# Upsampling matmuls on eight tiles of 32 rows by 64 columns, in staggered steps

## What is computed

```python
def _L1_conv_ref(input, bias, up_filter, down_filter):
    out = input + bias[None, :, None, None]
    out = _sep_upfirdn(out, up_filter * UP, UP, 1, UP_PAD)
    out = jax.nn.leaky_relu(out, NEG_SLOPE) * FLRELU_SCALE
    out = _sep_upfirdn(out, down_filter, 1, DOWN, DOWN_PAD)
```

## Time and profile before

| | |
|---|---|
| median of 3 runs | 7979.34 us (7979.21 to 7982.24) |
| profiled execution | 7980.32 us |
| its span, first to last instruction | 7978.5 us |
| mean granted TensorE clock | 0.959 of full speed |
| busy: PE, VectorE, ScalarE, POOL | 92%, 80%, 51%, 32% |
| resample stage | from about 1741 us to the end |

### The profile page before, as it was taken

The page is one execution under the profiler, slowest core; times in us unless marked ns, Lnnn a source line. Parts: engine busy times, 40 slices in busy tenths (PEclk is TensorE's granted clock), DMA queues, the critical chain, the costliest instruction groups (busy, mean ns, idle before and its releaser), DMA issues.

```text
span 7978.5 us, 374577 instructions
## 1 busy us (share of the span) xinstructions
PE 7350.8 (92%) x151493; PEld 6596.8 (83%) x151493; DVE 6373.1 (80%) x12643; ACT 4069.3 (51%) x8046; POOL 2543.3 (32%) x3076
## 2 busy tenths in 40 slices
PE   6888867049999999999999999999999999999999
PEld 3444442039999999999999999999999999999999
DVE  8999950878888888888888888888888888888887
ACT  0000002336666666666666666666666666666666
POOL 0000000014444444444344444444444444444443
PEclk9999978569999999999999999999999999999999
DMA  7777734013333333333333333333333333333332
GB/s 293 300 292 300 290 123 178 1 35 92 91 91 92 91 91 92 91 91 92 91 91 92 92 91 91 92 91 90 92 92 90 92 92 91 91 92 91 91 92 86
DMA packets 1253328, 925.41 MB, mean 116 GB/s; under 512 B 175312, under 2 KB 1224912, under 8 KB 1234384
## 3 DMA queue, kind: packets, MB, share of 16 engines
q1 hardware_dynamic: 1243920, 890.10, 34.4%
q10 hardware_dynamic: 9344, 34.61, 1.6%
HBM read 621.50 MB, written 303.04 MB: 116 GB/s over the span
## 4 chain that ended last, share of the span: by engine, by line
PE 78%; DVE 0%; ACT 0%; POOL 0%; issue 0%; DMA 0%; DVEq 0%; POOLq 0%
PE bank L991 38%; PE bank L980 29%; PE bank L985 9%; PE bank L1044 2%; DVE leaky L1152 0%; ACT slope_t L1091 0%; DMA low<-conv_dram 0%; POOL low_f L959 0%; DVE x_sum L1135 0%; ACT dn L1117 0%; POOL low_d L956 0%; POOL lift L962 0%; POOL img L947 0%; ACT low_v L1100 0%; ACT res L1108 0%
## 5 line engine op out<-in xcount | busy, mean ns | idle before, releaser
L1152 DVE SCALAR_TENSOR_TENSOR leaky<-bank,slope_t 128x512 f32<-128x512 f32 x4096 | 2637.2, 685 | 576.8 <-ACT slope_t L1091 512.5
L1091 ACT ACTIVATE slope_t<-bank 128x512 f32<-128x512 f32 x4096 | 2219.8, 597 | 1699.5 <-PE bank L985 1699.5
L980 PE MATMUL bank<-up_t,up 64*128 64x133 f32 x16384 | 2187.8, 273 | 2.1 <-DVE leaky L1152 1.9
L985 PE MATMUL bank<-up_t,up 64*128 64x133 f32 x16384 | 2188.1, 273 | 0.0
L991 PE MATMUL bank<-down_t,leaky 128*64 128x67 f32 x65536 | 2086.2, 222 | 0.0
L980 PEld LDWEIGHTS bank<-up_t,up 64*128 64x128 f32 x16384 | 2010.6, 187 | 3.1 <-issue 1.7
L985 PEld LDWEIGHTS bank<-up_t,up 64*128 64x128 f32 x16384 | 2007.9, 187 | 0.0
L991 PEld LDWEIGHTS bank<-down_t,leaky 128*64 128x64 f32 x65536 | 1999.0, 137 | 0.1
L1144 DVE COPY up<-bank 128x512 f32<-128x512 f32 x2048 | 1318.7, 685 | 628.1 <-PE bank L985 628.1
L956 POOL TENSOR_TENSOR low_d<-low_v 128x252 f32<-128x252 f32 x512 | 310.9, 607 | 4081.5 <-ACT low_v L1100 4081.5
L985 PE MATMUL bank<-up_t,x_sum 64*128 64x133 f32 x8192 | 1521.7, 299 | 0.0
(11 more groups left out here) (154 smaller groups left out, 3446.4 us busy)
## 6 DMA issues: line engine op xcount, KB each, us to landing
img<-in_x SPq DMA_DIRECT2D x1024, 256.0 KB, 2.8
out<-res SPq DMA_DIRECT2D x1024, 256.0 KB, 2.2
rows_in<-in_x SPq DMA_DIRECT2D x48, 4224.0 KB, 13.9
rows_in<-in_x SPq DMA_DIRECT2D x16, 4096.0 KB, 13.7
conv_dram<-conv ACTq DMA_DIRECT2D x64, 512.0 KB, 4.1
xb<-conv_dram SPq DMA_DIRECT2D x8, 4096.0 KB, 13.3
low<-conv_dram SPq DMA_DIRECT2D x512, 64.0 KB, 2.3
xx<-conv_dram SPq DMA_DIRECT2D x2, 2048.0 KB, 10.1
```

Of the source, the lines that this page charges most:

```text
L980: return pe.matmul(acc[:, 0:UP_REACH], src, up_t[0:HALF, 0:UP_REACH], start=first, stop=False, skip_group_check=True)
L985: return pe.matmul(acc[:, UH - UP_REACH:UH], src, up_t[HALF:P, UH - UP_REACH:UH], start=first, stop=False, skip_group_check=True)
L1091: nc.scalar.activation(slope_t[e][i][:], u2_acc[e][i][:], ACT.Copy, scale=SLOPE * GAIN).then_inc(slope_out, 1)
L1152: v.scalar_tensor_tensor(out=leaky[1 - m % 2][:, e, i].rearrange("p k w -> p (k w)"), in0=u2_acc[e][i][:], scalar=GAIN, in1=slope_t[e][i][ ...
```

## The change

Upsampling goes to eight tiles: four row tiles of 32 rows, each with two column tiles of 64. Row tile r reaches only the outputs from 2 x 32 r - 5 to 2 x 32 (r + 1) + 5, so 69 or 74 columns. The work of a slot is laid out as twelve steps: six items (two banks of the first upsampling, four of the second) with two halves each. In step t, row tile rt works on half-item (t - 3 rt) mod 12, so that the four row tiles are in four different banks. From step 2 on, a step waits for the end of the step before the last (`up_step`). The bilinear pass becomes two 64-column tiles over 128 rows, half of them zero, behind all of upsampling; d2_acc and b1_acc move to banks 1 and 7. The first downsampling of e = 0 goes ahead of the second downsampling. ScalarE takes over the copy of u1_acc[0]; slope_t of e = 0 goes ahead of low_v, and the copy stands behind all slope_t. On VectorE x_sum moves from the head of the slot to its end.

```diff
-UP_REACH = 2 * HALF + 5
+T = 32
+NT = P // T
+UP_REACH = [(max(0, 2 * T * r - 5), min(UH, 2 * T * (r + 1) + 5)) for r in range(NT)]
...
-                low = [sb(f"low{i}", [HO, LOWS, WO]) for i in range(2)]
+                low = [sb(f"low{i}", [P, LOWS, WO]) for i in range(2)]
...
-                d2_acc = bank[0]
-                b1_acc = bank[6][:, 0:LOWS * WO]
+                d2_acc = bank[1]
+                b1_acc = bank[7][:, 0:LOWS * WO]
...
+                ITEMS = ((1, 0), (2, 0, 0), (2, 1, 1), (2, 0, 1), (2, 1, 0), (1, 1))
+                STEPS = 2 * len(ITEMS)
...
+                    def rise(acc, src, rt, first):
+                        a, b = UP_REACH[rt]
+                        for c in range(2):
+                            mm = pe.matmul(acc[cols(c), a:b], src[:, cols(c)], up_t[T * rt:T * (rt + 1), a:b],
+                                           start=first, stop=False, skip_group_check=True)
+                        return mm
...
+                        used = set()
+                        for t in range(STEPS if has(u, 0) or has(u, 1) else 0):
+                            if t >= 2:
+
+                                pe.wait_ge(up_step, cnt(u, r, m, 0, per=STEPS) + (t - 1))
+                            for rt in range(NT):
+                                at = (t - 3 * rt) % STEPS
+                                item, half = ITEMS[at // 2], at % 2
+                                rows = slice(T * rt, T * (rt + 1))
+                                if item[0] == 1 and has(u, 0):
+                                    i = item[1]
+                                    if not used & {(1, 0), (1, 1)}:
+                                        pe.wait_ge(x_summed, cnt(u, r, m, 1))
...
+                                    mm = rise(u1_acc[i][:, half * UH:(half + 1) * UH], x_sum[p][rows, half, i, :], rt, item not in used)
+                                    used.add(item)
+                                if item[0] == 2 and has(u, 1):
+                                    e, i = item[1:]
+                                    if item not in used:
+
+                                        if i == 0:
+                                            pe.wait_ge(u1_out0, cnt(u, r, m, 0))
+                                        else:
+                                            pe.wait_ge(u1_out1, cnt(u, r, m, 0))
+                                        if after(u, 2):
+                                            pe.wait_ge(leaky_out, cnt(u, r, m, -2, per=4) + (2 * e + i + 1))
+                                    mm = rise(u2_acc[e][i][:, half * UW:(half + 1) * UW], up1[1 - p][rows, i, e, half * P:(half + 1) * P],
+                                              rt, item not in used)
+                                    used.add(item)
+                            mm.then_inc(up_step, 1)
...
+                            for c in range(2):
+                                mm = pe.matmul(b1_acc[cols(c)], const("lin")[:, cols(c)], low[(m // 2 + 1) % 2][:].rearrange("p c w -> p (c w)"),
+                                               start=True, stop=True)
+                            mm.then_inc(b1_mm, 1)
+                        if has(u, 2):
+                            pe.wait_ge(leaky_out, cnt(u, r, m, -1, per=4))
+                            if after(u, 3):
                                 pe.wait_ge(d1_out, cnt(u, r, m, -3, per=2) + 1)
...
+                            first_down(0, p)
...
-                            for e in range(2):
-                                first_down(e, p)
+                            first_down(1, p)
...
+                        if has(u, 0):
+                            act.wait_ge(up_step, cnt(u, r, m, 1, per=STEPS))
+                            nc.scalar.activation(up1[p][:, 0].rearrange("p e h -> p (e h)"), u1_acc[0][:], ACT.Copy).then_inc(u1_out0, 1)
...
+                    for i in range(2):
+                        v.memset(low[i][HO:P], 0.0).then_inc(padded, 1)
...
+                        if has(u, 0):
+                            v.wait_ge(up_step, cnt(u, r, m, 1, per=STEPS))
+                            v.tensor_copy(up1[m % 2][:, 1].rearrange("p e h -> p (e h)"), u1_acc[1][:]).then_inc(u1_out1, 1)
```

More of the change, by code:

```diff
@@ L976, in _ @@
                     pe.wait_ge(ready, 2 + 2 * FT)
-                    def upper(acc, src, first):
-                        return pe.matmul(acc[:, 0:UP_REACH], src, up_t[0:HALF, 0:UP_REACH],
-                                         start=first, stop=False, skip_group_check=True)
-                    def lower(acc, src, first):
-                        return pe.matmul(acc[:, UH - UP_REACH:UH], src, up_t[HALF:P, UH - UP_REACH:UH],
-                                         start=first, stop=False, skip_group_check=True)
+                    pe.wait_ge(padded, 2)
                     def down(acc, src, j, first):
@@ L994, in cols @@
                         return slice(HALF * c, HALF * (c + 1))
-                    def first_up(e, i, p, half, first):
-                        tile = (upper, lower)[half]
-                        return tile(u1_acc[i][:, e * UH:(e + 1) * UH], x_sum[p][HALF * half:HALF * (half + 1), e, i, :], first)
-                    def second_up(e, i, p, half, k, first):
-                        tile = (upper, lower)[half]
-                        return tile(u2_acc[e][i][:, k * UW:(k + 1) * UW],
-                                    up1[p][HALF * half:HALF * (half + 1), i, e, k * P:(k + 1) * P], first)
+                    def rise(acc, src, rt, first):
[4 more added lines that the diff above has]
+                        return mm
                     def first_down(e, p):
@@ L1028, in slot @@
-                        if has(u, 1):
-                            pe.wait_ge(u1_out, cnt(u, r, m, 0, per=2))
-                            for e in range(2):
-                                if after(u, 2):
-                                    pe.wait_ge(leaky_out, cnt(u, r, m, -2, per=4) + 2 * (e + 1))
-                                for k in range(2):
-                                    second_up(e, 0, 1 - p, 0, k, k == 0)
-                                    mm = second_up(e, 1, 1 - p, 1, k, k == 0)
-                            mm.then_inc(u2_half, 1)
+                        used = set()
@@ L1063, in slot @@
                             if has(u, 0):
[L1065 removed]
+                                pe.wait_ge(u1_out1, cnt(u, r, m, 1))
                             elif after(u, 4):
@@ L1075, in slot @@
                         if has(u, 2):
-                            pe.wait_ge(leaky_out, cnt(u, r, m, -1, per=4))
+                            if after(u, 3):
+                                pe.wait_ge(d1_out, cnt(u, r, m, -2, per=2))
                             if group:
                                 pe.wait_ge(b1_out, cnt(u, r, m, 4, of=2))
-                            for e in range(2):
-                                first_down(e, p)
+                            first_down(1, p)
                     schedule(pe, slot)
@@ L1094, in slot @@
                         p = m % 2
+                        if has(u, 1):
+                            act.wait_ge(up_step, cnt(u, r, m, 1, per=STEPS))
+                            slope(u, r, m, 0)
                         if m % 2 == 0 and has(u, -2):
@@ L1153, in slot @@
                                                            scalar=GAIN, in1=slope_t[e][i][:], op0=ALU.mult, op1=ALU.max).then_inc(leaky_out, 1)
+                        if has(u, -1):
+                            n = (m + 1) % STEP
+                            v.wait_ge(lifted, cnt(u, r, m, 1 + 2, of=2))
+                            v.wait_ge(biased, cnt(u, r, m, 2))
+                            for e in range(2):
+                                for i in range(2):
+                                    c0 = cnt(u, r, m, 1, per=4) + (2 * e + i)
+                                    cf = coef[:, bass.ds(c0, 1)] if u is None else coef[:, c0:c0 + 1]
+                                    ins = v.scalar_tensor_tensor(out=x_sum[n % 2][:, e, i, :], in0=lift[n // 2][:, 2 * (n % 2) + e, :],
+                                                                 scalar=cf, in1=img[n % 2][:, e, i, :], op0=ALU.mult, op1=ALU.add)
+                            ins.then_inc(x_summed, 1)
                     schedule(v, slot)
```

67 lines of the change are left out of this document (14 added, 53 removed).

## The result

The changed kernel takes 13,873.08 us (median, 13,851.46 to 13,929.94) against 7980.79 us for the kernel before beside it: ratio 1.739, with a 95% interval of 1.734 to 1.745. The forecast was 12,050 us with a range of 9,900 to 13,900. The direction and the likeliest case were right, the size is 1,820 us too small, and the time lies only 27 us inside the upper edge of the range; one of its four runs, at 13,930 us, lies outside.

A forecast was written before the change was run, and what follows sets the result against it. TensorE was taken to bound the kernel, and after the change the refetching of its loop body: 1782.7 us outside the loop + 16 straight-line + 254 rounds x 40.4 us = 12,060, predicted as 12,050 us, range 9,900 to 13,900.

The forecast's parts named there:

- the likeliest case: TensorE's loop: body fetched anew each round, rounds of 34.8 to 51.2 us, own range 10,600 to 13,900 us; chance 0.86.
- The body: TensorE's loop body grows to 2,400 instructions, touches 10 or 11 packets, doesn't fit and is fetched anew every round.
- Price of a packet: TensorE's instruction fetch: 3.2 us on demand, 3.1 to 3.7 us from one packet to the next, 3.4 taken.
- The round: Four pairs on TensorE: 6.4 us demand fetches, 2.6 cut packets, 29.4 whole packets, 2.0 x_sum; 40.4 us instead of 24.4.
- the clock as a risk at the upper edge: TensorE might fall to the lower clock while it starves for instructions, which lies at the range's upper edge.
- The order on VectorE: x_sum last in VectorE's slot: chain of 4.8 us, 1.7 us a pair unhidden; 0.5 a pair taken beside the fetches.
- rival B: TensorE's body stays held and the new x_sum chain sets the pace: 9,500 or 8,180 us; chance 0.11.
- The waits between steps: Upsampling on TensorE: two steps need at least 0.46 us, 0.23 each, 2.8 us for twelve, as much as now.
- the array's 1.5 us: Upsampling's lower bound, step wait always met: twelve steps in 1.5 us for 2.7, at best 1.2 us a pair less.
- the bound of 3.3 us: Upsampling's upper bound a pair: a further 0.05 us for every one of some 10 added register computations.
- Rival C: TensorE's body stays held and it runs at array speed: a round 19.7 us, 6,790 us in all; chance 0.02.
- What was costed at nothing: Other engines and order: ScalarE 17.6 us a round, VectorE 17.0, bilinear pass 0.43 as before, downsampling order with 2 us left.

The follow-up runs named there:

- b_body8: The kernel before, with TensorE's loop body at eight slots instead of four, 2,382 instructions for 1,194; 8,612 us, ratio 1.079.
- a_body2_xfirst: The changed kernel with TensorE's loop body at two slots (1,205 instructions) and x_sum back at the head of VectorE's slot; 8,459 us, ratio 1.060.
- b_xlast: The kernel before, with x_sum moved from the head of VectorE's slot to its end; 11,061 us, ratio 1.385.
- a_body2: The changed kernel with TensorE's loop body at two slots instead of four, 1,205 instructions, one low buffer; 10,855 us, ratio 1.359.
- a_waitprev: The changed kernel with two-slot body and x_sum at the head, each step waiting for the one just before it; 13,386 us, ratio 1.677.
- a_xfirst: The changed kernel with x_sum back at the head of VectorE's slot, four-slot body kept; 13,527 us, ratio 1.694.
- a_pool_early: Changed kernel, two-slot body, x_sum at head, step waits in mid-step, GpSimd's bias for two pairs before widening, img loaded before low; 8,054 us, ratio 1.009.

## Why the prediction was right, and where its size was off

**The body.** Right. The forecast 2,400 instructions are 2,407; 10 or 11 packets touched are 11 a round; about 2,800 packets and 45 MB are 2,819 and 46.19 MB. That the body is the cause is shown from both sides: with a short one the change has no packets and takes 3,018 us less, or 5,068 less with x_sum at the head (13,527 to 8,459), and the old kernel gets them with a long body. That the store is smaller than 11 packets was assumed with no row near 11, and it held; seven stay and eleven don't, and where between them the limit lies was not measured.

**Price of a packet.** The 3.2 us on demand fit: the first stall behind the branch has a median of 3.19 us (nine rounds in ten: 2.9 to 3.6) in the change and 3.6 in b_body8. The second stall is shorter, 1.9 us in the mean, behind some work between the two (1.32 us in the round shown). The 3.1 to 3.7 us from one packet to the next were too short: over the loop the middle interval is 3.96 us, only one in twenty is under 3.47, and 72% are over 3.7. In b_body8, where PE rarely stands, one interval in ten is under 3.1 us, so 3.5 is no floor of the fetch.

**The round** is the step that failed in size, 47.5 us for 40.4. The term was 8.4 whole packets at the longer of 3.4 us and what they run, 2.6 us on average, 3.9 in downsampling, both at full clock. By that term PE works 9.4 x 2.6 = 24.4 us a round and stands for 16.0. In the round shown it works 34.7 us and stands for 13.0. So the standing was put 3 us too high and the running 10 us too low, and part of the error cancelled.

PE's stalls brought the clock down to 0.77: downsampling's 96 instructions took 4.50 us, 256 at that pace 256 x 4.50/192 = 6.0 us, well over the 3.4 of a fetch. There a packet waits for PE and no longer PE for the packet. The same four pairs in a_body2_xfirst, at clock 1.00, have 2 x 13.08 x 0.987 = 25.8 us of busy PE. The other 8.9 us are slow running, 10.9 are "issue" (9.6 and 1.3) and 2.2 the wait for x_sum; the sum is 47.8, the round 47.67. The prediction named the clock as a risk at the upper edge and gave it no term. That the time still fell inside the range is in part luck, since no sum with the clock in it set the upper bound.

How much of the 8.9 us is the clock can be read from the windows of this round: the time from the branch to the first fall, then its three stretches at the lower level, 1.2 GHz.

```profile
7819.56:7825.62 6.06, 1.95 (x77) 1.69 (x74) 0.60 (x3) 1.32 (x3) 0.00 (x0) 1.00 0.37 103
...
7825.62:7835.86 10.24, 7.87 (x203) 6.84 (x204) 4.14 (x7) 2.85 (x6) 2.54 (x4) 0.50 0.01 3
7842.68:7846.10 3.42, 3.42 (x102) 3.23 (x92) 2.34 (x4) 2.28 (x5) 1.04 (x1) 0.50 0.02 5
7859.75:7866.58 6.83, 6.06 (x178) 5.51 (x172) 3.07 (x5) 2.56 (x5) 1.04 (x1) 0.50 0.12 34
```

PE stands for 4.1 of the first 6.1 us, and the price comes after it. It works for 17.35 us at half the clock, work of 8.7 us at full clock: 8.7 of the 8.9 us are the clock. What the round would take with its fetches and a full clock no run shows.

**The order on VectorE.** Right in kind, and the 4.8 us of the chain are 4.89 in b_xlast. The 0.5 us a pair that it was to add beside the fetches is 346/1024 = 0.34 (13,873 less 13,527). The 1.7 us that it would cost with the body held are 2,397/1024 = 2.3 on the change (10,855 less 8,459), and 3.0 on the kernel before, 1.1 of them in either case the clock. So rival B, given 9,500 us at the most, is really a_body2's 10,855: its idle time was sized well (1.6 us a pair), but not the clock that goes with it, nor a slower x_sum. The two losses don't add. Fetching alone costs 5,068 us, the chain alone 2,397, both 5,415 (13,873 less 8,459): the waits for x_sum lie mostly in the time in which a packet comes.

**The waits between steps.** 0.23 us a step was forecast, 0.25 measured; 2.8 us for twelve, 3.0. The choice of the semaphore bound over the array's 1.5 us was right, and a_waitprev shows its unit, 0.50 us for one way where 0.46 was the sum; the last matmul, put at 0.22 us in it, lasts 0.25 in a_body2_xfirst. But the reason given is only half of the truth: with two steps issued in between, 0.23 remain on average where the semaphore would allow 0.17. The 0.05 us for a register computation, from which the bound of 3.3 us came, had no row; upsampling stayed under it. Rival C at 6,790 us isn't near even with body and chain mended; 12 steps at 0.21 already give 2.5 us a pair and not 1.5.

**What was costed at nothing.** ScalarE is busy 17.09 us in the round shown, forecast 17.6. VectorE is busy 20.41 us, forecast 17.0. The difference is x_sum, 3.3 us (16 x 0.207), in its group on the page:

```profile
L1156 DVE SCALAR_TENSOR_TENSOR x_sum<-lift,coef,img 128x128 f32<-128x128 f32 x4096 | 2010.0, 550 | 7.6 <-POOL img L955 7.6
```

One took 343 ns before and takes 550 on average now, 347 in a_xfirst, 349 in a_body2_xfirst and 346 in b_xlast. So it is neither the place alone nor the tiling alone. The timelines of VectorE and of GpSimd in this round:

```profile
7832.41 2.57 DVE L1146 SCALAR_TENSOR_TENSOR leaky<-bank,slope_t 128x512 f32<-128x512 f32 x4
7834.89 2.81 DVE L1156 SCALAR_TENSOR_TENSOR x_sum<-lift,coef,img 128x128 f32<-128x128 f32 x4
...
7846.85 1.13 DVE L1156 SCALAR_TENSOR_TENSOR x_sum<-lift,coef,img 128x128 f32<-128x128 f32 x4
```

```profile
7835.14 1.10 POOL L970 TENSOR_TENSOR lift<-low_f,low_v 128x504 f32<-128x504 f32 x1
7836.20 1.09 POOL L955 TENSOR_TENSOR img<-img,bias_all 128x512 f32<-128x512 f32 x1
...
7842.88 1.04 POOL L955 TENSOR_TENSOR img<-img,bias_all 128x512 f32<-128x512 f32 x1 [5.59 <-DMA img<-in_x]
```

Four x_sum take 2.81 us while lift and img run, and 1.13 us when GpSimd has finished. From 4000 to 7000 us 378 of 1008 overlap GpSimd's work, with a mean of 0.90 us, and the other 630 have 0.34; in a_body2 some 550 of 1348 overlap, 0.82 and 0.34. In the traces of before, a_xfirst, b_xlast, a_body2_xfirst and a_pool_early none overlaps in that time, and all have 0.34 to 0.35. leaky isn't slowed: in the same time of the change 379 of 1010 overlap GpSimd, with 682 ns, and the others have 684. The Trainium skill ("SBUF — State Buffer", Who interferes with whom) has a VectorE instruction with two inputs from SBUF contend with a GpSimd instruction that reads SBUF, and not one with at most one SBUF input, outside two faster modes that the page names. x_sum has two, leaky one and an accumulator bank: the trace agrees.

**Small terms.** The bilinear pass, costed as before, was: it adds 0.48 us to its pair in a_body2_xfirst (from upsampling's last start to downsampling's first, 0.63 and not 0.15), and 0.45 before. What wasn't costed is the wait for VectorE's copy in the other pairs. There downsampling takes 3.19 us from its first start to its last, in pairs with a bilinear pass 2.75, and before 2.80 in both. So of the 0.44 us a pair by which a_body2_xfirst is above before (6.54 and 6.10) 0.3 are upsampling and 0.17 this wait. ScalarE's copy and the new order of downsampling weren't taken back by themselves. The prediction's "99% of each slice" says more than the page, whose slices say 90% or more; that PE was busy for all of the time is the earlier trace rows.

## What to carry to other kernels

Count the instructions of each engine's loop body, register computations and waits too, before splitting matmuls into more tiles; when a body grows past what a kernel is known to hold, measure what that costs on the old kernel by unrolling its loop further. Where an engine is about to wait, cost the wait and then the clock behind it: in this case 1.9 us of waiting a pair brought 1.1 us of slow running with it, and 0.25 us more a step cost 4,900 us in all. And an in-order engine's producer that is moved from the head of a slot to its end puts that whole slot into the loop's recurrence, even if no engine has more to do.

## What the runs showed of the hardware

- PE held a loop body of seven 16 KB instruction packets (1,789 instructions) and brought 11 in every round with a body of 2,382 or 2,407. Behind the branch it stood 3.2 us (median) with the change's code and 3.6 with the old, and in the change seven in ten packets followed the one before within 3.5 to 4.5 us.
- From PE to PE over a semaphore, with the issue of eight f32 matmuls of 69 to 74 columns, one way is 0.50 us. Eight 32 x 64 tiles in f32, 16 matmul instructions and 16 weight loads a step, took 0.23 us a step on average in the best version (0.16 to 0.39), and 2.70 us a pair, where two 64 x 128 tiles do the same work in 2.72.
- A chain of waits inside the matmuls that leaves PE "busy" for 89% brought its clock to 0.75, a kernel with 98.7% kept 1.00, and idle stretches of 1.9 us in each pair of 9 us gave 0.88. At the lower level PE's work took about twice as long: 4.59 us at a mean clock of 0.63 for what takes 2.9 at 1.00.
- A VectorE instruction of 128 x 128 f32 with two SBUF inputs took 0.82 to 0.90 us instead of 0.34 while GpSimd's additions ran, and one with an accumulator as its second input was not slowed.
